# Closing a row on TensorE: four matmuls of 128 nodes in place of eight of 64

## The reference

```python
h = jnp.maximum(_layernorm(x, axis=-1), 0.0)
for k in range(2):                                   # layer 0: sweeps 1 and 2
    agg = adj @ h
    h = jnp.tanh(jnp.concatenate([agg, h], axis=1) @ W0[k])
x = x + h
h = jnp.maximum(_layernorm(x, axis=-1), 0.0)
x = x + (adj @ (h @ weight) + bias)                  # layer 1: sweep 3
h = jnp.maximum(_layernorm(x, axis=-1), 0.0)
x = x + adj @ (h * (u >= 0.1) / 0.9)                 # layer 2: sweep 4
h = jnp.maximum(_layernorm(x, axis=-1), 0.0)
neigh = adj @ h / (adj.sum(axis=1, keepdims=True) + 1.0)
x = x + jnp.concatenate([h, neigh], axis=-1) @ W3.T  # layer 3: sweep 5
```

## Time and profile before

| | |
|---|---|
| Median of 3 runs | 2223.44 us (2221.93 to 2223.48) |
| Profiled execution, its own time | 2223.5 us |
| Its span | 2221.7 us |
| Mean granted TensorE clock | 0.999 |
| TensorE matmuls busy | 2186.6 us, 98% |
| TensorE weight loads busy | 1220.2 us, 55% |
| VectorE busy | 1734.6 us, 78% |
| ScalarE busy | 173.6 us, 8% |
| Matrix loads (q1) | 832.62 MB, 94.7% of 16 DMA engines |

### The profile page before, as it was taken

One profiled execution on the slowest core, in us unless ns is written; L12 is line 12 of the kernel. 1 busy time (PEld: TensorE's weight loads), 2 busy tenths in 40 slices (PEclk: granted clock), 3 DMA queues, 4 the chain that ended last, 5 costly groups with the idle time before them and its releaser, 6 DMA issues.

```text
span 2221.7 us, 37727 instructions
## 1 busy us (share of the span) xinstructions
PE 2186.6 (98%) x15686; PEld 1220.2 (55%) x15686; DVE 1734.6 (78%) x3316; ACT 173.6 (8%) x388; POOL 9.8 (0%) x22
## 2 busy tenths in 40 slices
PE   6999999999999999999999999999999999999999
PEld 3555555555554456677655667766344444444446
DVE  7467777777888888888766888887788877778776
ACT  1000000000002321111110000000100000000000
POOL 0000000000000000000000000000000000000000
PEclk9999999999999999999999999999999999999999
DMA  9999999999999878999999999999999999999997
GB/s 397 421 420 417 420 413 411 399 401 409 394 385 359 305 286 329 337 353 344 343 410 364 344 335 349 346 336 375 369 383 412 410 408 408 397 406 404 413 399 304
DMA packets 118762, 839.46 MB, mean 378 GB/s; under 512 B 14016, under 2 KB 16320, under 8 KB 17088
## 3 DMA queue, kind: packets, MB, share of 16 engines
q1 hardware_dynamic: 114480, 832.62, 94.7%
q10 hardware_dynamic: 3344, 2.33, 0.3%
q0 software_dynamic: 768, 2.10, 0.3%
HBM read 834.90 MB, written 2.10 MB: 377 GB/s over the span
## 4 chain that ended last, share of the span: by engine, by line
PE 91%; DVE 4%; DMA 2%; issue 1%; ACT 0%; SPq 0%; DVEq 0%
PE double_acc L917 35%; PE single_acc L945 19%; PE single_acc L889 16%; PE spare L917 14%; PE spare L889 7%; DMA store<-in_adj 2%; PE natural L1009 1%; DVE store L1356 1%; DVE stack L1275 1%; DVE store L1357 0%; ACT operand L1121 0%; DVE partial L1256 0%; DVE stats L1153 0%; PE spare L1022 0%; DVE store L1358 0%
## 5 line engine op out<-in xcount | busy, mean ns | idle before, releaser
L917 PE MATMUL double_acc<-store,operand 128*64 128x512 f32 x3856 | 859.7, 592 | 1.2 <-ACT operand L1121 1.2
L917 PEld LDWEIGHTS double_acc<-store,operand 128*64 128x64 f32 x3856 | 298.8, 137 | 459.1 <-issue 436.6
L889 PE MATMUL single_acc<-store,operand 128*64 128x256 f32 x3696 | 438.2, 381 | 21.7 <-DVE operand L1189 12.4
L945 PE MATMUL single_acc<-store 128*64 128x256 f32 x2368 | 456.8, 380 | 0.0
L945 PE MATMUL single_acc<-store,operand 128*64 128x256 f32 x1776 | 408.8, 380 | 5.0 <-DVE store L1358 5.0
L889 PEld LDWEIGHTS single_acc<-store,operand 128*64 128x64 f32 x3696 | 293.6, 137 | 188.7 <-issue 87.0
L917 PE MATMUL spare<-store,operand 128*64 128x512 f32 x1456 | 330.3, 592 | 0.6 <-DMA store<-in_adj 0.6
L945 PEld LDWEIGHTS single_acc<-store 128*64 128x64 f32 x2368 | 292.9, 137 | 56.6 <-issue 5.1
L945 PEld LDWEIGHTS single_acc<-store,operand 128*64 128x64 f32 x1776 | 241.9, 137 | 49.3 <-issue 11.5
L1256 DVE TENSOR_TENSOR partial<-spare,partial 64x256 f32<-64x256 f32 (+1 forms) x250 | 126.4, 506 | 172.0 <-PE spare L917 109.6
L917 PEld LDWEIGHTS spare<-store,operand 128*64 128x64 f32 x1456 | 125.7, 137 | 149.2 <-issue 141.5
(11 more groups left out here) (82 smaller groups left out, 902.8 us busy)
## 6 DMA issues: line engine op xcount, KB each, us to landing
store<-in_adj SPq DMA_DIRECT2D x792, 1024.0 KB, 8.2
for_layer<-in_u POOLq DMA_DIRECT2D x16, 128.0 KB, 6.0
out_rows<-resid ACTq DMA_DIRECT2D x15, 128.0 KB, 5.8
resid<-in_x SPq DMA_DIRECT2D x2, 512.0 KB, 6.0
resid<-in_x SPq DMA_DIRECT2D x1, 1024.0 KB, 13.6
out_rows<-resid ACTq DMA_DIRECT2D x2, 64.0 KB, 1.7
w_stack<-in_w_both ACTq DMA_DIRECT2D x2, 32.0 KB, 8.7
ident<-in_identity ACTq DMA_DIRECT2D x1, 64.0 KB, 16.4
```

The lines of the kernel that those rows point to most:

```text
L889: last = nc.tensor.matmul(acc[half_of(h), 0:HALF], operand[:, b.j * TPB + t, half_of(b.row.half)], stream[:, t, nodes_of(h)], start=b.firs ...
L917: last = nc.tensor.matmul(acc[half_of(half), :], operand[:, b.j * TPB + t, half_of(half)], stream[:, t, :], start=b.first and t == 0, stop ...
L945: last = nc.tensor.matmul(acc[half_of(half), nodes_of(nodes)], weights[:, t, :], data[:, t, :], start=first and k in (0, 2), stop=final an ...
```

## The change

For each of the four tiles of 128 nodes, the closing had two matmuls: 64 nodes as weights in columns 0 to 63, result to partitions 0 to 63 of the bank, and the next 64 nodes as weights in columns 64 to 127, result to partitions 64 to 127. Now one matmul has all 128 nodes as weights and writes all 128 partitions. The operands, the results and their places, the waits and the semaphores are the same.

```diff
                         last.then_inc(half_posted, 1)
                         wait_new(first_taken, rows_with_first(row.r))
                         acc = double_acc[0]
-                    for c in range(2):
-                        nodes = slice(t * P + c * F, t * P + (c + 1) * F)
-                        last = nc.tensor.matmul(acc[half_of(c), t * F:(t + 1) * F], stacked[:, nodes],
-                                                w_stack[:, row.sweep - 1, :], start=True, stop=True)
+                    last = nc.tensor.matmul(acc[:, t * F:(t + 1) * F], stacked[:, t * P:(t + 1) * P],
+                                            w_stack[:, row.sweep - 1, :], start=True, stop=True)
                 last.then_inc(posted, 1)
```

## The result

The changed kernel takes 2260.79 us (median of 4 runs, 2260.76 to 2260.83), against 2223.46 us (4 runs, 2221.93 to 2223.48). The ratio is 1.017, with an interval of 1.0158 to 1.0182. The change makes the kernel slower by 37.3 us; 41.4 were forecast. The profiled execution has a span of 2259.0 us, 37.3 more than before.

The account below looks back on a forecast made before the run. TensorE's instructions were taken to bound the kernel: 47 closings 33.8, row 14 0.7, six pairs 6.8 and the end 0.1 us make 41.4, so 2223.5 becomes 2264.9 us (71%), range 2247 to 2272.

Parts of the forecast that it names:

- The price of a closing: Row closing on TensorE: a lone one takes 1.18 us, 0.72 more than now.
- the rate: Closing's weight loads: a 128-column record starts every 0.11 us, so eight take 0.88 us in place of 0.46.
- the passage: Going from 64-column to 128-column matmuls and back around a closing costs 0.30 us, paid once for back-to-back closings.
- The pairs: Six pairs of back-to-back closings in the last sweep: 2.06 us each for 0.93, +1.13, together 6.8 us.
- What is hidden: Four closings between 696 and 1130 us cost nothing; row 15's hides 0.72 us; the last pair adds 0.1.
- these waits neither grow nor shrink for that reason: Turns of the sweeps: TensorE's waits for L1121, 1.2 us in three times, stay as they are.
- I leave it out of the sum: TensorE's clock, 1.00 in two long stretches and 0.98 in the last, was given no term.
- A: Closing: only the pace of weight loads counts, changing shape is free; +25, 2248.7 us; 13%.
- B: Closing: the shape-change cost grows with records, 0.16 us each; +53, 2276.6 us; 9%.
- C: Closing: time goes by number of records, 0.029 us each, saving 15.4 us: 2208 us; 3%.
- E: Closing: one full-width load keeps the present 0.0575 us pace and changing shape is free; no change; 2%.
- D: Matrix transfers set the pace, hiding 51 closings before 2170 us; 7.6 us left, 2231.1 us; 2%.

Follow-up runs that it names:

- two-wide kernels: Kernel before with two of each closing's four tiles as 128-node matmuls: adjacent (0 and 1) 2250.56 us, apart (0 and 2) 2268.04 us.
- the doubled one: Changed kernel with each closing matmul done twice, the last row once: 2316.47 us.
- group-by-group run: Kernel before with the eight closing matmuls reordered, all of column half 0 first, then half 1, last row apart: 2231.87 us.
- 128 columns streamed in the narrow shape: Kernel before, closing matmuls of sweeps 2 to 4 streaming 128 columns of w_stack in place of 64: 2235.15 us.
- four-group kernel: Kernel before with 16 closing matmuls of 32 nodes in four column groups, in place of eight of 64 in two: 2236.78 us.
- degree step in halves: Kernel before with the summing of degrees as six matmuls of 64 columns in two halves, in place of three of 128: 2220.65 us.
- two closings twice: Kernel before with the matmuls of the closings r = 21 and 22 done twice: ratio 0.9999.
- half 0 twice: Kernel before with column half 0's closing matmuls done once more in each tile, all rows but the last: 2250.04 us.
- its 128-column form: Changed kernel with closing matmuls of sweeps 2 to 4 streaming 128 columns of w_stack in place of 64: 2262.53 us.
- r = 22 four times: Closing at 779.64 us done four times: on the kernel before, ratio 0.9998; with the degree summing also in two column halves, 2219.06 us.

## Why the prediction was right, and by how much not

**The bound.** Right. TensorE's order of work is the kernel, and a longer closing is paid nearly wherever it stands: of 37.3 us, 22 closings in a row between 864.87 and 1539.49 give 15.8.

**The price of a closing.** Right in both terms: 8 x 0.11 = 0.88 for the rate and 0.30 for the passage, 1.18 us forecast and 1.18 read. Five degree steps were enough to price 67 closings, because they had the same shape. The two-wide kernels show the passage, and the doubled one the rate. The reason given for the rate, two halves that load side by side and one group of 128 that does not, holds. What failed was the expectation of the group-by-group run, that the halves overlap only when their instructions alternate: 2248 us expected, 2231.87 measured.

**The pairs.** 1.13 forecast, 1.14 read; five pairs added 5.4 rather than 5.7 between their lines, since two of the pairs before took 1.07 and 1.09 us and not 0.93.

**What is hidden.** The four closings in front of the waits for L1358 and row 15's were hidden as said. The wait for L1358 fell by 2.2 us (5.0 to 2.8): the second and third by 0.71 and 0.72, one closing each, but the first only from 2.76 to 1.91, by 0.85 and not the 1.44 of two closings. Another 0.34 went into the wait for L1409 ahead of the second of these two closings. Two places were missed. The first closing, at 57.3 us, stands in the start, where TensorE waits for its blocks (8.2 of DMA waits after, 9.2 before; the wait of 0.54 us right behind it, at 60.40, is gone), so 0.7 us less. And the step "these waits neither grow nor shrink for that reason", on the turns of the sweeps, was wrong: the table above has 0.75 us less at each of the turns to sweeps 2 and 4, 1.5 in all. The waits for L1121 fell from 1.2 to 0.6 us, those for L1409 from 2.1 to 1.4. Of the latter, in total before, and one of them before and after:

```profile
PE natural L1009 <- DVE stack L1409: 2.1, 4, 1.3
...
713.20 0.69 PE L1009 MATMUL natural<-w_stack,stack 128*64 128x64 f32 x16 [1.32 <-DVE stack L1409]
...
724.79 1.10 PE L1007 MATMUL natural<-w_stack,stack 128*128 128x64 f32 x8 [1.16 <-DVE stack L1407]
```

Three of the waits at the turns fell by 0.16 us each: this one, and two for L1121 (0.35 to 0.19 and 0.42 to 0.26). That is the size of the late block behind a closing, 0.15. In the kernels whose block behind is not late (group by group, 128 columns streamed in the narrow shape, two wide tiles together or apart) the three stay at 1.31 to 1.33, 0.34 to 0.35 and 0.41 to 0.43 us, although their closings are longer by 0.11 to 0.8 us; in the four-group kernel, whose closing also ends in another shape than the block behind it, they are 0.13 shorter each. So a longer closing leaves these waits as they were, as the prediction had it, but a late block behind it shortens them, and part of the passage is not paid there. My reading is that the users of a closing start when the closing is through, and the lateness of the block beside them costs them nothing. The wait ahead of the closing at 683.98 us (0.23 to nothing) and the first for L1121 (0.46 to 0.17) fell by more, and some 0.5 of the 1.5 us stands in no wait; their cause is open.

**The clock.** "I leave it out of the sum" cost 1.7 us. The wait of 2.76 us was in the rows, and behind it the clock had fallen in that execution; I looked at means over long stretches, where it did not show.

So 41.4 - 0.7 - 1.5 - 1.7 - 0.3 = 37.2 of the 37.3 measured, the 0.3 being the pairs. All four errors lie on the same side; none was made good by another. What part of the kernel's two levels is in the medians is bounded by the same 1.7 us: against the lower level the change costs 38.9 us.

**The rivals.** A (2248.7 us) falls by the two orders of wide tiles, B (2276.6) by the closing done twice, C and E by the 0.11 us step, D by the shifts in the table: TensorE's idle time fell by 6.1 us, more than the 4 expected, but only 1.0 of it was waiting for a DMA, at the start of the kernel. What C feared, or hoped, is true of no shape tried here: 32 records took no longer than 16 in the four-group kernel, so the count of instructions was not what a closing costs.

## What to carry to other kernels

Count a small fp32 matmul by the columns of weights and of stream that each column group has to take, not by instructions: half as many instructions with the full width took nearly twice the time (0.88 for 0.46 us), before the change of shape was paid. Before giving a step another width than its neighbours, look for any step in the trace that already has it, and price the change of shape from block start to block start, since 0.30 of the 0.72 us added lie in the late block behind it and the missed early load ahead of it. And where TensorE waits some microseconds for another engine, look at the granted clock in a window of 10 us around it: useless work in the wait can be free and keep the clock up.

## What the runs showed of the hardware that was not expected

- Column halves run on their own. In the group-by-group kernel the next block's first record (half 0) started at 1114.33 us, ahead of the last three records of the closing (half 1, from 1114.38). The page "TensorE: Matmul & The Clock Gate" of the Trainium skill, "Packing small matmuls", says that matmuls start and end strictly in order; the starts in this timeline are not in the program's order. The end of a record is modelled, so nothing is said here of ends.
- Going from 64-column to 32-column weights and back costs 0.28 us, nearly what going to 128 does (0.30). The drain that the page "TensorEngine Tiling (Array Packing)" of the Trainium skill, Key Properties, names for a change of mode agrees with both.
- The drop of the clock behind the wait near 795 us came in some executions and not in others of the same kernel. Behind a wait of 2.76 us it came in 16 of 21 and in 10 of 21 executions of the kernel before, and in 8 of 11 with the degree step in halves. Behind 2.28 us it came in 7 of 11 (two closings twice), and behind 2.3 to 2.6 us in 11 of 16 (group by group, half 0 twice, four groups, 128 columns in the narrow shape) and in none of 4 (two wide tiles together, 2.33 us). In the kernels with 1.91 us or less at this place (the changed kernel, its 128-column form, two wide tiles apart, and the two with r = 22 four times) it came in none of 34. The waits are those of one profiled execution of each kernel.
